# Routed experts in pieces of 64 tokens, two pieces to a 128-slot unit

## What is computed

```python
# layer 0: 16 experts, 2 picks for each token, and a shared expert
combine = jnp.sum(one_hot(topk_idx, E) * topk_w[..., None], axis=1)
gu = jnp.einsum('th,ehj->etj', x, w_gate_up)          # 256 -> 2 x 176
h = silu(gu[..., :I]) * gu[..., I:]
y = jnp.einsum('eti,eih,te->th', h, w_down, combine)  # 176 -> 256
y = y + swiglu(x @ shared_gate_up) @ shared_down
# layer 1: 8 experts, 1 pick for each token, no shared expert
out = jnp.einsum('eth,te->th', (silu(gate) * up) @ down, combine)
```

## Time and profile before

| | us |
|---|---|
| median of 3 runs | 724.89 |
| lowest and highest run | 722.25, 725.99 |
| span of the profiled execution, first to last instruction | 721.6 |
| the blocks of layer 0 on PE, first gate and up to last down | about 488.8 to 578.4 |
| the blocks of layer 1 on PE | about 673.4 to 717.6 |

### The profile page before, as it was taken

One profiled execution on the slowest core, in us unless ns is written; L12 is line 12 of the kernel. 1 busy time (PEld: TensorE's weight loads), 2 busy tenths in 40 slices (PEclk: granted clock), 3 DMA queues, 4 the chain that ended last, 5 costly groups with the idle time before them and its releaser, 6 DMA issues. The chain is left out here.

```text
span 721.6 us, 12441 instructions
## 1 busy us (share of the span) xinstructions
PE 659.8 (91%) x4222; PEld 553.4 (77%) x4222; DVE 405.8 (56%) x1063; ACT 340.2 (47%) x836; POOL 309.3 (43%) x377
## 2 busy tenths in 40 slices
PE   3888999999999999999999997889999968996997
PEld 3767888988988979979979896776666556986754
DVE  6758487196295295494493646783222269555343
ACT  2655766567467567566566561323343321200221
POOL 4565462552453444353351111616666315200563
PEclk9999999999999999999999999799999979995999
DMA  8011010110210200200100131993233162009440
GB/s 263 30 41 49 30 32 30 55 36 7 64 32 2 65 29 0 65 29 12 55 1 1 42 78 65 334 368 95 92 94 90 52 216 80 1 29 365 135 121 23
DMA packets 29778, 57.90 MB, mean 80 GB/s; under 512 B 4670, under 2 KB 15904, under 8 KB 29728
## 3 DMA queue, kind: packets, MB, share of 16 engines
q1 hardware_dynamic: 22720, 42.03, 17.1%
q0 software_dynamic: 4896, 13.12, 6.2%
q10 hardware_dynamic: 2112, 2.10, 0.8%
HBM read 48.06 MB, written 10.09 MB: 81 GB/s over the span
## 5 line engine op out<-in xcount | busy, mean ns | idle before, releaser
L911 DVE RECIPROCAL denominators<-readings 128x2 f32<-128x2 f32 x128 | 21.2, 166 | 147.6 <-PE readings L587 146.9
L447 POOL TENSOR_TENSOR w_high<-xn,ones 128x256 fp32r<-128x256 f32 x84 | 53.9, 672 | 76.7 <-PE ahead L235 35.5
L587 PEld LDWEIGHTS readings<-memory_copy,sigma 128*128 128x128 f32 x512 | 75.2, 191 | 11.2 <-ACT memory_copy L784 2.2
L793 ACT ACTIVATE memory_reading<-readings,denominators 64x128 f32<-64x128 f32 x256 | 78.7, 357 | 6.0 <-DVE denominators L911 4.0
L587 PE MATMUL readings<-memory_copy,sigma 128*128 128x129 f32 x512 | 78.8, 276 | 2.2 <-ACT memory_copy L784 2.1
L784 ACT ACTIVATE memory_copy<-memory 128x258 f32<-128x258 f32 x128 | 50.2, 392 | 61.9 <-PE memory L597 47.9
L917 DVE SCALAR_TENSOR_TENSOR minus_delta<-readings,denominators,v 64x128 f32<-64x128 f32 x240 | 73.8, 347 | 4.5 <-DVE denominators L911 0.3
L597 PE MATMUL memory<-minus_delta,sigma_k_tokens 128*128 128x129 f32 x480 | 73.2, 275 | 0.0
L1221 POOL DMA_INDIRECT xs_e<-rows_e,gather_at_e x46 | 44.6, 969 | 54.3 <-DVE gather_at_e L1635 19.0
L1368 PE MATMUL up_e<-weights_e,xT_e 128*128 x184 | 66.4, 483 | 1.2 <-ACT xT_e L1497 1.2
L451 POOL TENSOR_TENSOR w_low<-xn,w_high 128x256 fp32r<-128x256 f32 x84 | 65.7, 813 | 1.6
(11 more groups left out here) (282 smaller groups left out, 1444.6 us busy)
## 6 DMA issues: line engine op xcount, KB each, us to landing
weights_e<-experts SPq DMA_DIRECT2D x24, 608.0 KB, 12.1
xn<-L_attn_Wq SPq DMA_DIRECT2D x8, 512.0 KB, 3.9
xn<-L_attn_Wk SPq DMA_DIRECT2D x7, 512.0 KB, 3.8
xn<-L_attn_Wv SPq DMA_DIRECT2D x7, 512.0 KB, 3.8
wo<-L_attn_Wo SPq DMA_DIRECT2D x1, 2048.0 KB, 13.2
rows_e<-xn ACTq DMA_DIRECT2D x4, 512.0 KB, 10.4
x<-L_attn_x SPq DMA_DIRECT2D x4, 256.0 KB, 3.4
x<-L_attn_x SPq DMA_DIRECT2D x2, 512.0 KB, 3.5
```

The source lines that it names most:

```text
L447: last = pool.tensor_tensor(w_high[i][:, :, of], w_stage[:, :, of], one, ALU.mult)
L587: last = pe.matmul(KQ[g][:, hh * MC:(hh + 1) * MC], sqk[:, GROUP * g + hh, pair, 2 * par:2 * par + 2, :], mz[g][:, hh, :], start=True, sto ...
L793: last = act.activation(read[rows, half, GROUP * g + hh, pair, :], KQ[g][rows, hh * MC:hh * MC + DK], ACT.Copy, scale=nr[g][rows, hh:hh + 1])
```

## The change

Slots are now filled to multiples of 64 (GRAIN), and a unit of 128 slots holds two pieces of 64, which may belong to two experts. The bound on the units is half the number of pieces, rounded up: 24 in layer 0 and 12 in layer 1. Gathers, transposes, silu, gate and scatters still work on 128 slots.

The two products with weights are split in two: the 64 columns of the held operand that belong to the lower piece go to the lower half of PE's columns with the lower expert's weights, the other 64 to the upper half with the upper expert's. The stream has the same 352 or 256 columns for each half. All 128 rows of the second half of `hT` are used, where before 48 were. The upper expert's weights are first copied to a fixed place: DVE copies gate and up (128x704, `copy_gate_up`), ACT copies down (128x512, `copy_down`), each after loading `weight_at` into a register of its own. In layer 0 these copies lie in space that the shared expert's weights and hidden values have left.

Cut to what the prediction speaks of:

```diff
-    return (picks * T - experts) // P + experts
+    pieces = (picks * T - experts) // GRAIN + experts
+    return -(-pieces // PARTS)
...
             def block_gate_up(b, first):
                 pe.wait_ge(xt_copied, b + 1)
+                pe.wait_ge(gate_up_copied, b + 1)
                 if b >= 2:
                     pe.wait_ge(block_gated, b - 1)
                 for k in range(KD):
-                    last = pe.matmul(GU[b % 2][:, 0:2 * INTER], xT[b % 2][:, k, :],
-                                     flat[:, bass.ds(first + k * 2 * INTER, 2 * INTER)],
-                                     start=k == 0, stop=k == KD - 1)
+                    lower = flat[:, bass.ds(first + k * 2 * INTER, 2 * INTER)]
+                    upper = upper_gate_up[b % 2][:, k * 2 * INTER:(k + 1) * 2 * INTER]
+                    for half, moving in enumerate((lower, upper)):
+                        part = slice(half * GRAIN, (half + 1) * GRAIN)
+                        last = pe.matmul(GU[b % 2][part, 0:2 * INTER], xT[b % 2][:, k, part], moving,
+                                         start=k == 0, stop=k == KD - 1)
...
             def block_down(b, first):
                 pe.wait_ge(ht_copied, b + 1)
+                pe.wait_ge(down_copied, b + 1)
...
-                for k, count in enumerate((P, INTER - P)):
-                    last = pe.matmul(Y[b % 2][:, 0:D], hT[b % 2][0:count, k, :],
-                                     flat[0:count, bass.ds(first + 4 * INTER + k * D, D)],
-                                     start=k == 0, stop=k == 1)
+                for k in range(KD):
+                    lower = flat[:, bass.ds(first + 4 * INTER + k * D, D)]
+                    upper = upper_down[b % 2][:, k * D:(k + 1) * D]
+                    for half, moving in enumerate((lower, upper)):
+                        part = slice(half * GRAIN, (half + 1) * GRAIN)
+                        last = pe.matmul(Y[b % 2][part, 0:D], hT[b % 2][:, k, part], moving,
+                                         start=k == 0, stop=k == KD - 1)
...
+                if shared and b == 2:
+                    pe.wait_ge(added, 4)
+                if b >= 2:
+                    block_down(b - 2, firsts[b - 2])
                 if b + 2 < NB:
                     firsts[b + 2] = find_weights(b + 2)
                     turn_rows(b + 2)
                 if shared and b == 1:
-                    pe.wait_ge(added, 4)
+                    pe.wait_ge(added, 2)
                 if 0 <= b - 1 < NB:
                     turn_hidden(b - 1)
-                if b >= 2:
-                    block_down(b - 2, firsts[b - 2])
...
+            def copy_down(b):
+                first = act.value_load(weight_at[b:b + 1, 1:2], min_val=0, max_val=(E - 1) * WIDE)
+                if b >= 2:
+                    act.wait_ge(y_ready, b - 1)
+                act.activation(upper_down[b % 2][:, :], flat[:, bass.ds(first + 4 * INTER, 2 * D)], ACT.Copy)\
+                   .then_inc(down_copied, 1)
...
+            def copy_gate_up(b):
+                first = dve.value_load(weight_at[b:b + 1, 1:2], min_val=0, max_val=(E - 1) * WIDE)
+                if b >= 2:
+                    dve.wait_ge(gu_ready, b - 1)
+                dve.tensor_copy(upper_gate_up[b % 2][:, :], flat[:, bass.ds(first, 4 * INTER)])\
+                   .then_inc(gate_up_copied, 1)
...
+                copy_first()
                 find_slot_shares()
...
                 if 1 <= b <= NB:
                     copy_hidden(b - 1)
+                if b + 2 < NB:
+                    copy_gate_up(b + 2)
```

More of the change, by code:

```diff
@@ L53 @@
 WIDE = 2 * 2 * INTER + 2 * D
+GRAIN = 64
+PARTS = P // GRAIN
 LARGE = 1e30
 def blocks_of(experts, picks):
-    return (picks * T - experts) // P + experts
+    pieces = (picks * T - experts) // GRAIN + experts
+    return -(-pieces // PARTS)
 def table_columns(experts, picks):
     at, begin = {}, 0
-    for name, n in (("upper", P), ("lane", P), ("full", NT), ("earlier", experts * experts),
+    for name, n in (("upper", P), ("lane", P), ("full", T // GRAIN), ("earlier", experts * experts),
                     ("block", blocks_of(experts, picks)), ("row", 1), ("tile", picks * NT),
-                    ("spare", blocks_of(experts, picks)), ("rank", experts), ("one", 1), ("first", 1)):
+                    ("spare", blocks_of(experts, picks)), ("rank", experts), ("one", 1), ("first", PARTS)):
         at[name] = begin, begin + n
@@ L1078, in sparse_layer @@
         key, total, inverse = sb("key", [P, NT]), sb("total", [P, NT]), sb("inverse", [P, NT])
-        over, blocks_e = sb("over", [P, E, NT]), sb("blocks_e", [P, E])
+        over, blocks_e = sb("over", [P, E, T // GRAIN]), sb("blocks_e", [P, E])
         before, begin = sb("before", [P, E, E]), sb("begin", [P, E])
@@ L1098, in sparse_layer @@
         ys = [sb(f"ys{i}", [P, D]) for i in range(RING)]
+        if shared:
+            upper_gate_up = [carried.upper_gate_up, stage[2][:, :, :].rearrange("p i d -> p (i d)")[:, 0:4 * INTER]]
+            upper_down = [carried.upper_down, sg[0]]
+        else:
+            upper_gate_up = [sb(f"upper_gate_up{i}", [P, 4 * INTER]) for i in range(2)]
+            upper_down = [sb(f"upper_down{i}", [P, 2 * D]) for i in range(2)]
         if out is None:
@@ L1515, in retention_high @@
                    .then_inc(carried.w_high_done, 1)
+            def copy_down(b):
[4 more added lines that the diff above has]
+                   .then_inc(down_copied, 1)
             copy_rows(0)
             copy_rows(1)
+            act.wait_ge(experts_ready, 1)
+            act.wait_ge(weights_loaded, 16 * E)
+            if shared:
+                act.wait_ge(split_done, 2)
+                act.wait_ge(h1_done, LAST)
             for b in range(NB + 2):
@@ L1525, in _ @@
                     copy_result(b - 2)
+                if b < NB:
+                    copy_down(b)
                 if shared and b in SPLIT_AT:
@@ L1575, in first_slots @@
                 dve.wait_ge(counted, 1)
-                step(dve.tensor_tensor(over[:, :, :], R[:, COUNTS + NT * E:COUNTS + (NT + 1) * E].unsqueeze(2).to_broadcast([P, E, NT]),
-                                       const("full").unsqueeze(1).to_broadcast([P, E, NT]), ALU.is_gt))
+                step(dve.tensor_tensor(over[:, :, :], R[:, COUNTS + NT * E:COUNTS + (NT + 1) * E].unsqueeze(2).to_broadcast([P, E, T // GRAIN]),
+                                       const("full").unsqueeze(1).to_broadcast([P, E, T // GRAIN]), ALU.is_gt))
                 step(dve.tensor_reduce(blocks_e[:, :], over[:, :, :], AX.X, ALU.add))
@@ L1647, in find_experts, with copy_first @@
             def find_experts():
-                step(dve.scalar_tensor_tensor(out=end[:, :], in0=blocks_e[:, :], scalar=float(P), in1=begin[:, :],
+                step(dve.scalar_tensor_tensor(out=end[:, :], in0=blocks_e[:, :], scalar=float(GRAIN), in1=begin[:, :],
                                               op0=ALU.mult, op1=ALU.add))
-                step(dve.tensor_scalar(ended[:, :], end[:, :], const("first"), None, ALU.is_le))
-                step(dve.tensor_reduce(expert_f[:, :], ended[:, :], AX.X, ALU.add))
+                step(dve.tensor_tensor(ended[:, :, :], end[:, :].unsqueeze(1).to_broadcast([P, PARTS, E]),
+                                       const("first").unsqueeze(2).to_broadcast([P, PARTS, E]), ALU.is_le))
+                step(dve.tensor_reduce(expert_f[:, :], ended[:, :, :], AX.X, ALU.add))
                 dve.tensor_scalar(weight_at[:, :], expert_f[:, :], float(E - 1), float(WIDE), ALU.min, ALU.mult)\
                    .then_inc(experts_ready, 1)
+            def copy_gate_up(b):
[4 more added lines that the diff above has]
+                   .then_inc(gate_up_copied, 1)
+            def copy_first():
+                dve.wait_ge(experts_ready, 1)
+                dve.wait_ge(weights_loaded, 16 * E)
+                if shared:
+                    dve.wait_ge(split_done, 3)
+                copy_gate_up(0)
+                copy_gate_up(1)
             def hidden(n):
@@ L2064, in routing_table @@
         "lane": np.tile(lane, (P, 1)),
-        "full": np.tile(P * np.arange(NT), (P, 1)),
-        "earlier": np.tile((P * (np.arange(experts)[None, :] < np.arange(experts)[:, None])).reshape(-1), (P, 1)),
+        "full": np.tile(GRAIN * np.arange(T // GRAIN), (P, 1)),
+        "earlier": np.tile((GRAIN * (np.arange(experts)[None, :] < np.arange(experts)[:, None])).reshape(-1), (P, 1)),
         "block": np.tile(P * np.arange(nb), (P, 1)),
@@ L2072, in routing_table @@
         "one": np.ones((P, 1)),
-        "first": P * lane[:, None],
+        "first": P * lane[:, None] + GRAIN * np.arange(PARTS)[None, :],
     }
```

6 lines of the change are left out of this document (4 added, 2 removed).

## The result

The changed kernel takes 696.4 us (median of 4 runs, 695.1 to 697.0), the kernel before beside it 724.8 (4 runs, 722.3 to 726.0): a ratio of 0.962, with a 95% interval of 0.959 to 0.964. Forecast were 695.4, with 689 to 712 as the range. The profiled run took 696.3 us, its span 694.5.

The account below looks back on a forecast made before the run. PE was taken to bound the kernel. Layer 0's -21.5, layer 1's -9.4 and the ends' +1.4 gave -29.5, taken from 724.9: 695.4 us, main case 690 to 701 (0.70), wider range 689 to 712.

Parts of the forecast that it names:

- The bound and its unit: Expert units in both layers: PE sets the pace, and a unit takes 2.82 us (2.79 to 2.84) against a block's 2.877.
- a block without changes of shape: A block of the kernel before, 2.877 us, less 0.394 for its two changes to 48 rows and back.
- the halves' two changes: Into the column halves before gate and up, out behind down: 0.29 to 0.34 us a unit together, taken as 0.32.
- the second half's 0.013: In gate and up and down: 0.013 us added in a unit for the half that comes second.
- The overlap: Gate and up and down: a pair for both column halves costs what one product does, inferred from the attention's L608.
- (b): Rival on the paired products: the halves overlap only in part, +0.25 to +0.31 us a unit, 706 us; chance 0.07.
- (c): Rival on the paired products: the halves do not overlap, +2.05 us a unit, 769 us, slower than before; chance 0.05.
- two changes a unit: In PE's pass: a unit has two changes of shape, since down now stands next to gate and up.
- The copies: Upper expert's weights on DVE (0.59 us) and ACT (0.62 us): they hide behind PE and cost nothing.
- Rival (a): In the units: the copies or the waits on them set the pace, about 707 us (700 to 716); chance 0.16.
- The moved product: Down of b-2, moved ahead in PE's queue, waits for its hidden copy; this hides with 0.6 to 0.7 us cover.
- The ends: Each layer's last down waits some 0.3 us, and layer 1's third unit comes 0.8 later: +1.4 us together.

Follow-up runs that it names:

- e_one_half: The changed kernel, with the upper piece's products also written to the lower column half from each layer's third unit on: 763.4 us, 1.054 of before.
- e_down_last: The changed kernel, with PE's order within a pass as before the change, down behind both transposes: 695.3 us, 0.962 of before.
- e_copies_twice: The changed kernel, with each of the two copies of the upper expert's weights made twice, one behind the other: 698.7 us, 0.969 of before.
- e_ends: The changed kernel, with the last hidden values turned ahead of the last but one's down, and the third unit's weights copied before DVE's first gate: 694.0 us.
- e_lower_first: The changed kernel, with each unit's two lower-half products issued first and then its two upper-half ones, instead of by turns: 698.0 us, 0.964 of before.
- e_whole_width: The changed kernel, with each unit's 128 columns multiplied by the lower piece's weights over the whole array, no column halves: 686.7 us, 0.948 of before.

## Why the prediction was right, point by point

**The bound and its unit.** That PE sets the pace held in the units of every run above. The unit was put at 2.82 (2.79 to 2.84) and measured 2.785. Its parts: a block without changes of shape 2.877 - 0.394 = 2.483, measured 2.486 in two kernels; the halves' two changes 0.29 to 0.34, taken as 0.32, measured 0.30; the second half's 0.013, measured as 0.005 to 0.012 between the starts of a pair. The changes were priced from single steps in another stage and from a line's longest durations, and their pieces came out too: into the halves 0.093 + 0.048 = 0.141, measured 0.15, out of them 0.15 to 0.20, measured 0.15, and each change of the rows 0.197, measured 0.20, although its 0.093 was borrowed from a change of the columns.

**The overlap.** From L608's 1.75 full overlap was inferred for long streams. It held. Most of what L608 loses is its start: in the trace its last 17 starts lie 0.029 us apart, 0.058 a pair, where the prediction's estimate for one such product alone is 0.055. Rivals (b) and (c) are refuted by e_one_half, which gives the full 2.04 back.

**The reason given for two changes a unit was wrong.** The step says that a unit has two "since down now stands next to gate and up". In the loop it stood next to it before as well, at the other side (e_down_last). The number of changes was right, but the move has nothing to do with it, so the term came out right by luck. What the move does is to open gaps at the ends.

**The copies.** Estimated 0.59 for DVE's, measured 0.527 (median of L1701); ACT's 0.62 against 0.63 (L1544). Cost in the steady state: nothing, with over 0.5 us to spare on each engine. Rival (a) falls with e_copies_twice.

```profile
L1701 DVE COPY carried<-weights_e x12: 526/527/599, 487.0 to 548.1; 128x704 f32 x12
L1544 ACT ACTIVATE carried<-weights_e x12: 629/632/633, 493.0 to 553.1; 128x512 f32 x12
```

**The moved product.** The cover was put at 0.6 to 0.7. In the unit shown above, DVE's copy of hidden values starts at 516.71 and ends at 517.13, and down follows at 517.84: 0.71.

**The ends were mis-sized.** The sum has one gap of 0.3 in each layer. There are two of 0.60 in each: the last but one's down stands right behind the turning of its own hidden values, and the turning of the last hidden values waits in PE's queue behind that down. In layer 0:

```profile
555.82 0.43 PE L1406 MATMUL down_e<-weights_e,hT_e 128*64 x1 [0.60 <-DVE hT_e L1796]
...
557.88 0.42 PE L1406 MATMUL down_e<-weights_e,hT_e 128*64 x1 [0.60 <-DVE hT_e L1796]
```

That is 2.4 us in both layers, not 0.6. For layer 1's third unit the sum has +0.8; from the first gate and up to the third were 4.51 us before and 5.46 after, so +0.95. Here the profile names the wrong releaser:

```profile
658.45 0.53 DVE L1701 COPY upper_gate_up_e<-weights_e 128x704 f32 x1 [0.41 <-PE up_e L1384]
...
659.20 0.51 PE L1384 MATMUL up_e<-weights_e,xT_e 128*64 x1 [0.58 <-ACT xT_e L1518]
```

ACT's copy of the rows (starting at 657.46, 0.38 long) had long been done; DVE's copy ended at 658.98, 0.22 ahead of PE's start, and e_ends, which puts that copy first, brought the start forward by 0.66. So 0.66 of the 0.95 was the copy.

**How the sum closed.** The units gained more than forecast, 24 x 2.785 - 89.2 = -22.4 and 12 x 2.785 - 43.2 = -9.8, 1.3 us together; the ends lost 4.0 (what is left to the stage's -28.2) where 1.4 was put. The gaps make 2.4 of that and layer 1's third unit 0.95; the other 0.65 has no row here. The stage came to -28.2 against -29.5. The span forecast was 692.1 and is 694.5: 1.3 of the difference is the stage, 1.1 lies outside it. That the time is so near the forecast has two pieces of luck in it. The units' gain and the ends' loss, each mis-sized, make up for each other in part. And the profiled run stands 1.8 over its span, where 3.3 was taken, the median of the runs before less the span of one that lay under it; with 1.8 the forecast would have been 693.9.

## What to carry to other kernels

Where a product uses only half of the array's columns, two of them for different halves cost what one does, as they did here with 352 and 256 columns streamed, and nearly so in either order of issue; but count the changes of shape around the loop, its last step next to its first, at the 0.30 us measured here for each time in and out, and put work of one shape together. Before packing, look for a shape that changes by accident: here 48 rows in place of 128 cost 17 us, and padding with zeros gave it back. And a product that is moved ahead in an in-order queue takes its wait with it: look at the ends of the loop, where nothing stands behind it to fill the gap.

## What the runs showed that was not expected

- The two column halves take their products independently of the order in the program: issued behind both of the lower half's products, the upper half's first still starts 0.01 us after the lower half's first. The cost of the other order was 0.05 us a unit.
- A change between 128 and 48 rows and back costs 0.39 us, more than one between the whole array and the column halves, 0.30.
- The granted clock differs from run to run at one place, the start of layer 0's units: it was 0.50 for some us in e_lower_first, e_whole_width and e_copies_twice, and 1.00 in the changed kernel and its seven other variants, with the same program ahead of it. From 480 to 487 us PE had been busy for 5.3 us in e_lower_first, where the clock fell, and for 4.8 in the changed kernel, where it didn't; these rows don't say why. At the lower level the first gate and up took 2.75 us instead of 1.40. A stage's start is not comparable to better than that.
- Turning rows and hidden values within the halves as well would save the last changes. That wasn't tried. The Trainium skill says in TensorEngine Tiling (Array Packing), Restrictions, that column tiling excludes transposes of such 32-bit data; no run here shows it.
